# Spreading the reciprocals of the cross-attention sums with one float32r product of two parts

## The reference, cut to what matters

```
# layer 0: 16 heads of 8 channels, with a mask; layer 1: 8 heads of 16 channels
scores = einsum('bhqc,bhkc->bhqk', q, k) / sqrt(channels)
p_attn = softmax(scores, axis=-1)
out    = einsum('bhqk,bhkc->bhqc', p_attn, v)
out    = einsum('oi,bit->bot', wo, out) + bo      # layer 0 only
x      = layernorm(x + out)
```

## Time and profile before

| | us |
|---|---|
| median of 3 runs | 1685.72 |
| lowest and highest | 1685.56, 1687.22 |
| span of the profiled execution | 1684.2 |
| TensorE busy | 1400.9 (83%) |
| VectorE busy | 982.0 (58%) |
| ScalarE busy | 609.2 (36%) |
| GpSimd busy | 419.8 (25%) |
| mean granted TensorE clock | 0.926 of full |

### The profile page before, as it was taken

One profiled execution on the slowest core, in us unless ns is written; L12 is line 12 of the kernel. 1 busy time (PEld: TensorE's weight loads), 2 busy tenths in 40 slices (PEclk: granted clock), 3 DMA queues, 4 the chain that ended last, 5 costly groups with the idle time before them and its releaser, 6 DMA issues. The chain is left out here.

```text
span 1684.2 us, 29387 instructions
## 1 busy us (share of the span) xinstructions
PE 1400.9 (83%) x9221; PEld 874.6 (52%) x9331; DVE 982.0 (58%) x2623; ACT 609.2 (36%) x1389; POOL 419.8 (25%) x588
## 2 busy tenths in 40 slices
PE   2478999999999954899999946588888875999997
PEld 1245565665665522466566524455555543566654
DVE  5467788787777624222222224577788651676775
ACT  0123444544544421223222223255566542232321
POOL 2242342342341101011111023455555310000000
PEclk9679999999999976999999976799999996999999
DMA  3233443333432106611111123745454311100000
GB/s 91 59 66 60 70 72 52 72 70 55 72 67 37 24 27 226 225 32 38 32 32 33 28 56 109 159 105 114 107 116 111 85 34 50 38 1 13 13 1 26
DMA packets 165337, 112.77 MB, mean 67 GB/s; under 512 B 32690, under 2 KB 155826, under 8 KB 165056
## 3 DMA queue, kind: packets, MB, share of 16 engines
q1 hardware_dynamic: 150272, 99.04, 26.1%
q0 software_dynamic: 3408, 9.31, 2.3%
q10 hardware_dynamic: 11504, 2.53, 0.8%
HBM read 46.48 MB, written 12.45 MB: 35 GB/s over the span
## 5 line engine op out<-in xcount | busy, mean ns | idle before, releaser
L892 ACT ACTIVATE first_probs<-pair 128x512 f32<-128x512 f32 x320 | 189.0, 598 | 231.0 <-PE pair L408 217.4
L449 DVE TENSOR_REDUCE first_negmax_x<-bank 128x2 f32<-128x512 f32 x256 | 177.1, 692 | 59.7 <-PE bank L393 39.8
L393 PE MATMUL bank<-kept_stack_cross 96*128 96x256 bf16 x768 | 151.9, 280 | 11.8 <-DMA kept_stack_cross<-second_parts_x_q 7.5
L1885 ACT ACTIVATE second_probs<-pair 128x512 f32<-128x512 f32 x192 | 113.7, 598 | 130.8 <-PE pair L408 111.6
L408 PE MATMUL pair<-kept_stack_cross 98*128 98x256 bf16 x768 | 148.1, 275 | 3.0 <-ACT first_probs L892 1.0
L1439 PE MATMUL pair<-kept_w,experts_hidden_t 128*128 x312 | 140.5, 593 | 0.0
L449 DVE TENSOR_REDUCE second_negmax_x<-bank 128x2 f32<-128x512 f32 x128 | 88.6, 692 | 59.6 <-PE bank L393 50.5
L393 PEld LDWEIGHTS bank<-kept_stack_cross 96*128 96x128 bf16 x768 | 74.4, 102 | 73.0 <-issue 21.6
L1480 ACT ACTIVATE experts_hidden_t<-bank,kept_b 128x128 f32<-128x128 f32 x156 | 44.6, 368 | 186.4 <-PE bank L1414 186.4
L1394 POOL DMA_INDIRECT experts_expert_rows<-x_mid,kept_row_of x39 | 37.2, 953 | 275.6 <-PE bank L1406 249.1
L386 PE MATMUL bank<-kept_mask_q,kept_ident 128*128 128x512 bf16 x221 | 86.4, 391 | 20.4 <-DVE first_negmax_x L449 11.8
(11 more groups left out here) (430 smaller groups left out, 2947.2 us busy)
## 6 DMA issues: line engine op xcount, KB each, us to landing
kept_stack_self<-first_parts_a SPq DMA_DIRECT2D x128, 64.0 KB
kept_w<-in_L_ffn_W SPq DMA_DIRECT2D x16, 512.0 KB, 9.1
kept_w<-in_L_ffn_W SPq DMA_DIRECT2D x8, 1024.0 KB, 9.5
kept_stack_self<-second_parts_a SPq DMA_DIRECT2D x128, 64.0 KB
kept_stack_cross<-first_parts_x_k SPq DMA_DIRECT2D x96, 64.0 KB
kept_stack_cross<-first_parts_x_q SPq DMA_DIRECT2D x96, 64.0 KB
kept_stack_cross<-second_parts_x_k SPq DMA_DIRECT2D x96, 64.0 KB
kept_stack_cross<-second_parts_x_q SPq DMA_DIRECT2D x96, 64.0 KB
```

What stands on the lines that cost most here:

```text
L393: mm = pe.matmul(out, q, k, start=mask is None, stop=True, skip_group_check=True)
L449: return dve.tensor_reduce(negmax[:, 2 * n:2 * n + 2], bank[:, :].rearrange("p (m t) -> p m t", t=D), AX.X, ALU.max, negate=True)
L892: act.activation(probs[i % RING][:, :], key_bank[i % 2][:, :], ACT.Exp, scale=att.scale).then_inc(probs_made, 1)
L1885: act.activation(probs[i % RING][:, :], key_bank[i % 2][:, :], ACT.Exp, scale=att.scale).then_inc(probs_made, 1)
```

## The change

The reciprocals no longer go back into `heads_x`. VectorE splits each into a high part, rounded to float32r, and the low rest. Two DMAs write them into two neighbouring rows of each block of a new tile `spread` (128x512, float32r) that is cleared once per stage. The constant matrices have ones in both rows and are float32r too, so that one float32r product adds the parts and spreads them. `sum_of` is made by eight additions of two columns in place of eight copies, and `sum_of1` by a copy of a loaded tile. The waits count 32 instead of 16 for each batch. The second stage's edits are the same with YC, 32 and SUMS.

```diff
-        sum_of[p // 32 * 32 + YC, p] = 1.0
+        sum_of[p // 32 * 32 + YC:p // 32 * 32 + YC + 2, p] = 1.0
...
-        loads += [(t["sum_of1"][:, :], d["c_sum_of"]), (t["by_row"][:, :, :], d["c_by_row"])]
+        loads += [(sum_raw[:, :], d["c_sum_of"]), (t["by_row"][:, :, :], d["c_by_row"])]
...
-                at = t["ident"][:, 16 * n + XC:16 * n + XC + 1].unsqueeze(2).broadcast_to([P, 1, 16])
-                dve.tensor_copy(t["sum_of"][:, 16 * n:16 * n + 16].unsqueeze(1), at)
+                at = [t["ident"][:, 16 * n + c:16 * n + c + 1].unsqueeze(2).broadcast_to([P, 1, 16]) for c in (XC, XC + 1)]
+                dve.tensor_tensor(t["sum_of"][:, 16 * n:16 * n + 16].unsqueeze(1), at[0], at[1], ALU.add)
+            dve.tensor_copy(t["sum_of1"][:, :], sum_raw[:, :])
...
+        recip_parts, spread = [sb(f"recip_{part}", [P, 32], F32R) for part in ("high", "low")], sb("spread", [P, XG // SHARED * D], F32R)
...
-                pe.wait_ge(recips_laid, 16 * (b + 1))
-                pe.matmul(small_bank[:, :], t["sum_of"][:, :], heads_x[:, :], start=True, stop=True).then_inc(sums_spread, 1)
+                pe.wait_ge(recips_laid, 32 * (b + 1))
+                pe.matmul(small_bank[:, :], t["sum_of"][:, :], spread[:, :], start=True, stop=True).then_inc(sums_spread, 1)
...
             def lay_recips(b):
+                if b == 0:
+                    act.wait_ge(spread_cleared, 1)
                 act.wait_ge(recips_made, b + 1)
-                act.dma_start(heads_x[XC:P:16, :], recips[:, :]).then_inc(recips_laid, 16)
+                for n in range(2):
+                    act.dma_start(spread[XC + n:P:16, :].bitcast(F32), recip_parts[n][:, :].bitcast(F32)).then_inc(recips_laid, 16)
...
-                    dve.wait_ge(recips_laid, 16 * b)
-                dve.reciprocal(recips[:, :], sums[:, :]).then_inc(recips_made, 1)
+                    dve.wait_ge(recips_laid, 32 * b)
+                dve.reciprocal(recips[:, :], sums[:, :])
+                dve.drain()
+                dve.tensor_copy(recip_parts[0][:, :], recips[:, :])
+                dve.drain()
+                dve.tensor_tensor(recip_parts[1][:, :], recips[:, :], recip_parts[0][:, :].bitcast(F32), ALU.subtract).then_inc(recips_made, 1)
...
             for two in (two_a, two_x):
                 dve.memset(two[:, :], 0.0)
+            dve.memset(spread[:, :].bitcast(F32), 0.0).then_inc(spread_cleared, 1)
...
-            ... ("sum_of", [P, P], F32), ("sum_of1", [P, P], F32) ...
+            ... ("sum_of", [P, P], F32R), ("sum_of1", [P, P], F32R) ...
```

More of the change, by code:

```diff
@@ L9 @@
 BF16 = mybir.dt.bfloat16
+F32R = mybir.dt.float32r
 I32 = mybir.dt.int32
@@ L133, in prepare_weights @@
         ones_row = sb("ones_row_bf", [P, 2, 512], BF16)
+        sum_raw = sb("sum_raw", [P, P])
         first_loaded, loaded, rest_made = sem("first_weights_loaded"), sem("weights_loaded"), sem("rest_made")
@@ L582, in first_layer_attentions @@
         out_copied, out_turned, sums_spread = sem("out_copied"), sem("out_turned"), sem("sums_spread")
-        sums_laid, recips_made, recips_laid = sem("sums_laid"), sem("recips_made"), sem("recips_laid")
+        sums_laid, recips_made, recips_laid, spread_cleared = sem("sums_laid"), sem("recips_made"), sem("recips_laid"), sem("spread_cleared")
         out_x_copied, heads_x_made, y_made, sum_x_made = sem("out_x_copied"), sem("heads_x_made"), sem("y_made"), sem("sum_x_made")
@@ L1564, in second_layer_attentions @@
         sums, recips = sb("sums", [P, SUMS]), sb("recips", [P, SUMS])
+        recip_parts, spread = [sb(f"recip_{part}", [P, SUMS], F32R) for part in ("high", "low")], sb("spread", [P, YG // GROUP * D], F32R)
         sum_a, sum_x = sb("sum_a", [P, D]), sb("sum_x", [P, D])
@@ L1595, in second_layer_attentions @@
         parts_q_made, parts_k_made, kv_turned, xv_copied = sem("parts_q_made"), sem("parts_k_made"), sem("kv_turned"), sem("xv_copied")
-        out_x_copied, sums_laid, recips_made, recips_laid, sums_spread = (
-            sem(n) for n in ("out_x_copied", "sums_laid", "recips_made", "recips_laid", "sums_spread"))
+        out_x_copied, sums_laid, recips_made, recips_laid, sums_spread, spread_cleared = (
+            sem(n) for n in ("out_x_copied", "sums_laid", "recips_made", "recips_laid", "sums_spread", "spread_cleared"))
         heads_x_made, y_made, sum_x_made, x5_made, x5_turned, x5_copied, queries_made, queries_copied = (
@@ L1804, in spread_sums @@
             def spread_sums(b):
-                pe.wait_ge(recips_laid, 16 * (b + 1))
-                pe.matmul(out_x[:, :], t["sum_of1"][:, :], heads_x[:, :], start=True, stop=True).then_inc(sums_spread, 1)
+                pe.wait_ge(recips_laid, 32 * (b + 1))
+                pe.matmul(out_x[:, :], t["sum_of1"][:, :], spread[:, :], start=True, stop=True).then_inc(sums_spread, 1)
             def make_y(b):
@@ L1962, in lay_recips @@
             def lay_recips(b):
+                if b == 0:
+                    act.wait_ge(spread_cleared, 1)
                 act.wait_ge(recips_made, b + 1)
-                act.dma_start(heads_x[YC:P:32, :], recips[:, :]).then_inc(recips_laid, 16)
+                for n in range(2):
+                    act.dma_start(spread[YC + n:P:32, :].bitcast(F32), recip_parts[n][:, :].bitcast(F32)).then_inc(recips_laid, 16)
             def copy_x5(b):
```

2 lines of the change are left out of this document (1 added, 1 removed).

## The result

| | before | changed |
|---|---|---|
| median us | 1686.47 (1685.56 to 1697.22, 4 runs) | 1710.11 (1705.71 to 1713.1, 4 runs) |
| ratio, 95% interval | 1 | 1.0133 [1.0105, 1.0161] |
| span of the profiled execution | 1684.2 | 1703.9 |
| VectorE busy | 982.0 | 1003.1 |
| TensorE busy | 1400.9 | 1392.6 |

Before's median is now over a fourth run, 1697.22 us, besides the three of the table ahead of the prediction. The change makes the kernel about 22 us slower, where 8.9 us less was forecast. TensorE did get less to do and VectorE more; the difference is idle time of TensorE.

What follows compares the result with a forecast made beforehand. TensorE was taken to set the first stage's pace almost alone, the second's with short waits on other engines. First stage -4.2, second -5.0, preparation +0.3 gave -8.9 us: median 1676.8 us, 8-in-10 range 1671 to 1684.5.

Steps and rivals of the forecast that it cites:

- The product: TensorE's spreading product, both stages: one float32r pass in place of float32, 0.64 us saved each, 1.28 at half clock.
- the first rival: Second stage's ten steady batches: the gain turns into another wait and gives 0; about 1683 us; chance 0.18.
- VectorE in the second stage: Copy and subtraction, 0.52 us a batch, covered by VectorE idle of 0.25 and 0.81: nothing; without cover 0.52 a batch.
- VectorE in the first stage: Copy and subtraction ahead of the query rotation: 0.52 us on TensorE's path in seven batches, 0.22 in four.
- The stage's ends: Last batches of both stages: 1.10 us added to the chain, 0.64 or 1.28 saved: +0.46 or -0.2 each.
- The second DMA: One more 0.58 us issue on ScalarE a batch: hidden in the first stage, 0.13 a batch in the second.
- The rival of the low part that lands late: TensorE waits at the second stage's spreading product: +1.1 us in ten batches, +7 in all, 1693; chance 0.06.
- The rival on the slow side: The low part's late landing at the second stage's spreading product, later scores queued behind: +7, 1693 us; chance 0.06.
- The third rival: Spreading product gets no cheaper as float32r, so the costs stand alone: +13.6, 1699 us; chance 0.06.
- Preparation: Ahead of the stages: one more 128x128 copy, +0.3 us; the small additions and the clearing of the new tile cost nothing.

Runs made afterwards that it cites:

- B: VectorE's split of the reciprocals (copy, subtraction, drains), compared on and off in four pairs of kernels: mean ratio change +0.0127 (+21 us).
- e1: Kernel before plus VectorE's copy and subtraction into tiles nobody reads, float32 product and one DMA kept: 1716.04 us, ratio 1.0163.
- four pairs: Kernels with and without one part (float32r product, split, second DMA), the other two parts alike: mean ratio changes -0.0050, +0.0127, +0.0034 respectively.
- e7: Changed kernel plus eight bf16 products ahead of TensorE's wait for the reciprocals in the second stage's last five batches: 1706.08 us, ratio 1.0104.
- e8: Kernel before plus six bf16 products ahead of TensorE's wait for the reciprocals in the second stage's last five batches: 1681.89 us, ratio 0.997.
- e10: Changed kernel with the high part made by a second reciprocal from the sums, one drain and the cast dropped: 1702.68 us, ratio 1.0089.

## Why the prediction was wrong

- **The product** was right in size (0.64 us forecast, 0.54 to 0.61 saved a product). What it is worth was not: of about 22 us of product time that the sum took out in all, about 8 arrived: 4 to 8 us in the first stage, of about 10, and some in the second's end. In the second's steady part the first rival, the gain that turns into another wait, is what the runs show (6.1 us less work, 4.9 us more waiting).
- **VectorE in the second stage, costed at nothing, is the step that failed.** The sum counted the idle 0.25 and 0.81 us behind the reciprocal as cover and said that the maximum that TensorE needs there is not the late one. Waits for the maxima rose from 1.2 to 6.3 us. VectorE's list runs in order, so everything behind the split, the layer norm's steps, the casts and the next maxima, is pushed, and idle that VectorE spends waiting for TensorE's next scores is not free: TensorE waits for VectorE's answer in turn. B costs 6 to 12 us in this stretch alone. "If that cover were gone it would be 0.52 a batch" gives 5, and that is the waiting that e1 shows, 0.49 a batch. The other half of e1's 10.5 us is the clock, which the sum left out in the steady batches: three more batches run in part at 1.2 GHz.
- **VectorE in the first stage** was the right mechanism at the wrong size: 4.5 us in the sum, where the wait at the keys' product grew by 6.3 and the four pairs give 7 to 12. The row that priced the steps (0.26 us each) stands where GpSimd runs nothing; at the reciprocal, GpSimd is in a 1.16 us instruction (399.10 to 400.26 in the trace of before), and in the changed kernel the cast waits for that instruction's end: 0.85 us for the two steps. So this wait grew by 0.93 us to 1.33, where the prediction looked for 0.9 in all, and +3.9 us stand in place of -4.
- **The stage's ends.** The waits were right. The sum had 1.10 us more chain in each of the last three batches; measured were 1.70, 0.79 and 0.78, 1.09 on average. From the eleventh batch's product to the last one it adds up to 4.6 us more waiting (0.7, 0.58 and three times 1.10), and TensorE's idle time grew by 4.9. What it lacked is the clock: it priced the product at half clock but not that more of the *other* products would run at 1.2 GHz. TensorE should have been busy 3.8 us less there and was busy 3.3 us more, so +8.1 stands in place of about +0.8.
- **The second DMA** was nearly right in steady batches (+1.3 us forecast, +2.2, +3.8, -2.1 and -0.8 in four pairs). Over the whole kernel it was not: 6 us on average of the four pairs, the most of it in the second stage's end. The rival of the low part that lands late did not come true there: L1819 waits for it only in the stages' ends.
- **The rival on the slow side** priced the wrong place. The loss is no late transfer in the steady batches, but all that stands behind the split in VectorE's list, each a little late, and with it the clock. The third rival's sum (1699) needed an unchanged product, which the trace excludes.
- **Preparation**: nothing to see, as forecast (the first product of the first stage starts 0.7 us earlier).

Open is what the split would cost in another slot of VectorE's list: moving it wasn't tried. Nor was the clock held up in the steady batches by products ahead of their waits, as e7 and e8 do in the end, so that the longer waits there lower the clock is read from the traces and not shown by a run.

## What to carry to other kernels

An engine's idle time covers an insertion only if the idle ends in something nobody waits for; where two engines pass work back and forth through two banks, half a microsecond inserted into one is paid by the other, each batch. Price an inserted instruction at its place, beside what the other engines do there. And count the clock with it: here longer waits of TensorE went with a lower clock, in single steady batches and above all at the stage's end, where spare products ahead of the wait paid for themselves.

## What was not expected of the hardware

- A float32r product of 128x128 with 128x512 leaves one record of 0.47 to 0.50 us at full clock, with the next start 0.32 us behind it in the second stage and 0.57 in the first; the float32 product leaves two, and 0.86 and 1.18 us.
- Some short VectorE instructions are held to the end of GpSimd's: a cast of 128x32 took 0.51 us in place of 0.18, a subtraction of 128x32 in e10 0.37 in place of 0.19. A reciprocal of 128x32 into float32r beside the same GpSimd instruction (e10) took 0.29 there as in the batches without it, so it was not held.
- The TENSOR_SCALAR of 128x256 that makes `second_x` was at times held over an indirect DMA's instruction on GpSimd and the tensor_tensor behind it. Of all its places beside such an instruction in the 14 traces, it took 1.8 to 2.1 us in 13 of the 14 where it began 0.21 us or more behind that instruction's start, and 0.40 to 0.46 us wherever it began earlier. Which of the two counts, the late start or what GpSimd does next, is not shown.
- Six bf16 products more a batch, 30 in all, made the second stage's end 1.6 us shorter in the kernel before, with the clock at 0.98 in place of 0.91 (e8). Products that compute nothing can shorten a stretch.
